# Sums of P and V of four tiles in one slot, with four buffers of transposed P, and the second attention's next y turned ahead of the output projection

## The reference

```python
x = x + xattn(ctx_1024, _layernorm(x), mask, ...)   # 16 batches, 64 latents, 512 context rows
x = x + attn(_layernorm(x), ...)                     # differential attention within each batch
x = x + ffn(_layernorm(x), ...)                      # block-quantised to FP4, inner width 1408

# xattn, width 512, 8 heads of 64: keys and values from context and latents
q = ln @ w_q
k, v = split(concatenate([xn, ln], axis=1) @ w_kv)
attn = softmax(where(m, einsum('bhid,bhjd->bhij', q, k), -max))
out = _ln(einsum('bhij,bhjd->bhid', attn, v) @ w_out, g_o, b_o)
# attn: q and k with rotary positions, two softmaxes per head
o = o1 - lam * o2
o = o * rsqrt(mean(o*o) + EPS) * ln_w + ln_b
out = o.reshape(b, s, e) @ Wo.T
```

## Time and profile before

| | |
|---|---|
| median of 3 runs | 959.94 us (958.75, 959.94, 959.97) |
| profiled execution, its own time | 958.88 us |
| its span | 957.1 us |
| busy: PE, DVE, ACT, POOL | 942.2 (98%), 730.1 (76%), 522.4 (55%), 142.7 us (15%) |
| mean granted PE clock | 0.999 of full speed |
| chain that ended last | PE 85%, DVE 6%, ACT 4%, DMA 2% |

### The profile page before, as it was taken

How to read it: one execution, slowest core, us unless ns; L and a number is a source line. 1 busy time by engine, 2 the same in 40 slices (tenths; PEclk the granted TensorE clock), 3 DMA queues, 4 the chain that set the end, 5 groups by cost and what they waited for, 6 DMA issues and landing times.

```text
span 957.1 us, 16824 instructions
## 1 busy us (share of the span) xinstructions
PE 942.2 (98%) x6400; PEld 777.4 (81%) x6400; DVE 730.1 (76%) x1512; ACT 522.4 (55%) x1088; POOL 142.7 (15%) x175
## 2 busy tenths in 40 slices
PE   9999999999999999999999999999999999999997
PEld 8778888888888888888888888776776778888885
DVE  6636577788787887886886854778898788999985
ACT  4535777777687777777776874623343422222221
POOL 6420101101201210111012010132231100000000
PEclk9999999999999999999999999999999999999999
DMA  6687657655675565676567535090004940000000
GB/s 223 167 280 209 200 135 192 158 130 157 166 185 131 163 152 154 155 196 149 129 147 181 157 106 161 12 242 2 1 1 118 247 121 12 11 12 12 12 12 23
DMA packets 119453, 120.07 MB, mean 125 GB/s; under 512 B 47430, under 2 KB 88070, under 8 KB 117324
## 3 DMA queue, kind: packets, MB, share of 16 engines
q1 hardware_dynamic: 111980, 93.30, 37.3%
q0 software_dynamic: 6816, 24.64, 8.3%
q10 hardware_dynamic: 576, 1.05, 0.3%
HBM read 89.04 MB, written 29.93 MB: 124 GB/s over the span
## 4 chain that ended last, share of the span: by engine, by line
PE 85%; DVE 6%; ACT 4%; DMA 2%; SPq 1%; issue 1%; POOL 0%; DVEq 0%; ACTq 0%; POOLq 0%
PE ps_banks L147 21%; PE ps_banks L148 21%; PE ps_banks L149 21%; PE ps_banks L473 6%; PE ps_banks L605 4%; PE ps_banks L686 3%; PE ps_banks L755 2%; PE ps_banks L756 2%; PE ps_banks L757 2%; SPq L132 1%; DMA sb_w_out_raw<-in_w_out 1%; DMA sb_wdn<-scratch_wdn 1%; PE ps_banks L486 1%; PE ps_banks L589 1%; PE ps_banks L651 1%
## 5 line engine op out<-in xcount | busy, mean ns | idle before, releaser
L147 PE MATMUL ps_banks<-sb_zT_hi,sb_wkv_hi 128*128 128x512 f32 x256 | 104.7, 409 | 0.0
L148 PE MATMUL ps_banks<-sb_wkv_lo,sb_zT_hi 128*128 128x512 f32 x256 | 100.4, 392 | 0.0
L147 PE MATMUL ps_banks<-sb_wkv_hi,sb_zT_hi 128*128 128x512 f32 x256 | 100.4, 392 | 0.0
L149 PE MATMUL ps_banks<-sb_zT_hi,sb_wkv_lo 128*128 128x512 f32 x256 | 100.3, 392 | 0.0
L149 PE MATMUL ps_banks<-sb_wkv_hi,sb_zT_lo 128*128 128x512 f32 x256 | 100.0, 391 | 0.0
L148 PE MATMUL ps_banks<-sb_zT_lo,sb_wkv_hi 128*128 128x512 f32 x256 | 99.9, 390 | 0.0
L987 DVE CUSTOM_DVE_ANT_0 sb_probs<-ps_banks,sb_maskbias 128x576 f32<-128x576 f32 x64 | 48.2, 754 | 41.5 <-PE ps_banks L149 39.9
L936 DVE TENSOR_TENSOR sb_kfull<-ps_banks,sb_rstd_row 128x512 f32<-128x512 f32 x64 | 44.2, 690 | 44.2 <-PE ps_banks L149 44.2
L1466 ACT ACTIVATE sb_kT_hi<-sb_kfull 128x512 fp32r<-128x512 f32 x64 | 40.5, 632 | 65.2 <-DVE sb_kfull L936 64.4
L147 PE MATMUL ps_banks<-sb_wgu,sb_z_hi 128*128 128x512 f32 (+1 forms) x192 | 74.0, 385 | 0.0
L148 PE MATMUL ps_banks<-sb_wgu,sb_z_hi 128*128 128x512 f32 (+1 forms) x192 | 72.1, 376 | 0.0
(11 more groups left out here) (275 smaller groups left out, 2520.8 us busy)
## 6 DMA issues: line engine op xcount, KB each, us to landing
sb_ctx<-in_ctx SPq DMA_DIRECT2D x16, 1024.0 KB, 6.4
sb_ctxT<-in_ctx_t SPq DMA_DIRECT2D x16, 1024.0 KB, 6.1
scratch_wgu<-sb_w_both POOLq DMA_DIRECT2D x22, 512.0 KB, 5.5
sb_wgu<-scratch_wgu SPq DMA_DIRECT2D x44, 256.0 KB, 5.0
sb_wdn<-scratch_wdn SPq DMA_DIRECT2D x8, 704.0 KB, 8.5
scratch_q<-sb_a_qk POOLq DMA_DIRECT2D x8, 512.0 KB, 6.6
sb_rstd_row<-scratch_rstd SPq DMA_DIRECT2D x16, 256.0 KB, 4.3
sb_qpack<-scratch_q SPq DMA_DIRECT2D x32, 128.0 KB, 6.2
```

Source lines behind the costliest of these rows:

```text
L147: e.matmul(o, wh, xh, start=i == 0, stop=False)
L148: e.matmul(o, wh, xl, start=False, stop=False)
L149: m = e.matmul(o, wl, xh, start=False, stop=i == n - 1)
```

## The change

Five things change. The program has the same multiplications, the same DMAs, and two more memsets on POOL.

1. `weigh_v` of all four tiles of the batch before is issued in slot 3. Transposed P has four buffers, with four for the latents' part.
2. The room for them comes from other buffers: `k_full` is single, so that `scale_k` waits for the `lo_of_k` before it; the quantised weight is written over `xn`, so that step 3 instead of step 10 of the next job waits for PE's transposes; two pairs of statistics buffers are shared.
3. `out_split` (DVE, even batches) stands ahead of the quantisation steps of slot 5.
4. In the second attention `turn_y(k + 1)` moves for k = 2 to 6 from step D to the place directly ahead of `project_o`. `hi_of_y` on ACT then follows `copy_out`, `lo_of_y` on DVE follows `combine`, and ACT's `copy_qk(k, 0)` stands one step later for every k.
5. `turn_a(0)` stands behind `project(2, 0)`.

```diff
-        k_full = [sb(stage_b, f"kfull{i}", [P, S]) for i in range(2)]
+        k_full = sb(stage_b, "kfull", [P, S])
+        p_main = [None, None, sb(stage_b, "probsT2", [P, CS, P]), None]
...
-        w_q4 = sb(stage_b, "w_q4", [P, D])
+        p_main[3] = sb(stage_b, "probsT3", [P, CS, P])
...
+        w_q4 = quant_w[3]
...
@@ PE, attention()
-                    if old:
+                    if old and k != 2:
                         turn_a(k - 2)
                     if new:
                         project(k, 0)
+                    if k == 2:
+                        turn_a(0)
...
-                    if k + 1 < NT:
+                    if k < 2:
                         turn_y(k + 1)
...
+                    if old and k + 1 < NT:
+                        turn_y(k + 1)
                     yield
                     if old and k != NT:
                         project_o(k - 2)
@@ PE, batches
-                    if old and slot == 0:
-                        weigh_v(b - 1, 0)
-                        weigh_v(b - 1, 1)
                     if old and slot == 3:
-                        weigh_v(b - 1, 2)
-                        weigh_v(b - 1, 3)
+                        for n in range(C):
+                            weigh_v(b - 1, n)
@@ DVE
-                if idx >= 2:
-                    on.wait_ge(k_split, idx - 1)
+                if idx:
+                    on.wait_ge(k_split, idx)
...
-                        if step == QUANT_STEPS - 1 and job:
+                        if step == 3 and job:
                             taken(("w", job - 1))
...
                     if mid:
                         combine(k - 1)
+                    if old and k + 1 < NT:
+                        lo_of_y(k + 1)
...
+                    if t_new is not None and slot == 5:
+                        out_split(t_new)
@@ ACT, copy_p and copy_p_latents
-                if idx >= 2:
-                    on.wait_ge(v_weighed, idx - 1)
+                if b:
+                    on.wait_ge(v_weighed, C * (b - 1) + n + 1)
@@ ACT, attention()
                     if new:
                         copy_v_d(k)
-                        copy_qk(k, 0)
                     yield
                     if old:
                         copy_out(k - 2)
+                    if old and k + 1 < NT:
+                        hi_of_y(k + 1)
                     if new:
+                        copy_qk(k, 0)
                         copy_qk(k, 1)
```

More of the change, by code:

```diff
@@ L216, in perceiver @@
         lam = sb(ctx, "lam", [P, 8])
-        small_z = ln_small(ctx, "e", NT)
         small_o, small_y = ln_small(ctx, "lo", NT), ln_small(ctx, "ly", NT)
-        small_b = ln_small(ctx, "b", CS)
+        small_z = (small_y[0], sb(ctx, "e_mv", [P, NT, 2]), sb(ctx, "e_ve", [P, NT]), sb(ctx, "e_rstd", [P, NT]))
+        small_b = (small_o[0], sb(ctx, "b_mv", [P, CS, 2]), sb(ctx, "b_ve", [P, CS]), sb(ctx, "b_rstd", [P, CS]))
         rstd_b = sb(ctx, "rstd_b", [P, 2, CS])
@@ L269, in perceiver @@
         probs = [sb(stage_b, f"probs{i}", [P, S + LQ]) for i in range(2)]
-        p_t = [sb(stage_b, f"probsT{i}", [P, CS + 1, P]) for i in range(2)]
+        p_whole = [sb(stage_b, f"probsT{i}", [P, CS + 1, P]) for i in range(2)]
         mask_in = [sb(stage_b, f"mask{i}", [P, S], U8) for i in range(2)]
@@ L283, in perceiver @@
         quant_w = quant_small(stage_b, "wq4", D)
+        w_q4 = quant_w[3]
         rstd_row = sb(stage_b, "rstd_row", [P, S])
+        p_latent = [sb(stage_b, f"probsT_l{i}", [P, P]) for i in (2, 3)]
+        p_main = [p[:, 0:CS, :] for p in p_whole] + [p[:, :, :] for p in p_main[2:]]
+        p_latent = [p[:, CS, :] for p in p_whole] + [p[:, :] for p in p_latent]
         stage_b.close()
@@ L301, in perceiver @@
         w_d_lo[0], w_d_lo[1] = (sb(stage_d, f"dw{n}_lo", [P, C, D], F32R) for n in "qk")
-        y = [sb(stage_d, f"y{i}", [P, D]) for i in range(2)]
+        y = [sb(stage_d, "y0", [P, D]), None]
+        leave(2048)
         w_d_lo[2] = sb(stage_d, "dwv_lo", [P, C, D], F32R)
@@ L310, in perceiver @@
         e_sb = [sb(stage_d, f"e_sb{i}", [P, 2 * H, LQ]) for i in range(2)]
-        leave(2048)
+        y[1] = sb(stage_d, "y1", [P, D])
         w_d_hi[0] = sb(stage_d, "dwq_hi", [P, C, D], F32R)
@@ L592, in weigh_v @@
             def weigh_v(b, n):
-                i, j = b % 2, n % 2
+                i = b % 2
                 on.wait_ge(drained[took["p", b, n][0]], took["p", b, n][1])
@@ L604, in weigh_v @@
                         value = vl_pack[i][:, vs] if k == CS else v_sb[i][:, k, vs]
-                        m = e.matmul(o_space(r, n), value, p_t[j][:, k, r], start=k == CS, stop=k == CS - 1)
+                        p = p_latent[n][:, r] if k == CS else p_main[n][:, k, r]
+                        m = e.matmul(o_space(r, n), value, p, start=k == CS, stop=k == CS - 1)
                 m.then_inc(v_weighed)
@@ L933, in scale_k @@
                 on.wait_ge(w_folded, 2 * C)
-                if idx >= 2:
-                    on.wait_ge(k_split, idx - 1)
-                e.tensor_tensor(k_full[n % 2][:, :], psum[:, bank, :], rstd_row[:, :], ALU.mult).then_inc(drained[bank])
+                if idx:
+                    on.wait_ge(k_split, idx)
+                e.tensor_tensor(k_full[:, :], psum[:, bank, :], rstd_row[:, :], ALU.mult).then_inc(drained[bank])
             def lo_of_k(b, n):
-                split_lo(k_full[n % 2][:, :], k_hi[:, n, context_keys], k_lo[:, n, context_keys], k_hi_done, C * b + n + 1, k_split)
+                split_lo(k_full[:, :], k_hi[:, n, context_keys], k_lo[:, n, context_keys], k_hi_done, C * b + n + 1, k_split)
             def batch_stats(b):
@@ L1371, in vector_program @@
                         lo_of_z(b + 1, slot - 4)
-                    if t_new is not None and slot == 5:
-                        out_split(t_new)
                     if cur and slot < 4:
@@ L1545, in hi_of_k @@
                     on.wait_ge(scored, C * (b - 1) + n + 1)
-                copy(k_hi[:, n, context_keys], k_full[n % 2][:, :], k_hi_done)
+                copy(k_hi[:, n, context_keys], k_full[:, :], k_hi_done)
             def copy_v(b, k):
@@ L1567, in copy_p @@
             def copy_p(b, n):
-                j, idx = n % 2, C * b + n
                 bank = taken(("p", b, n))
-                if idx >= 2:
-                    on.wait_ge(v_weighed, idx - 1)
-                copy(p_t[j][:, 0:CS, :].rearrange("p c n -> p (c n)"), psum[:, bank, :], drained[bank])
+                if b:
+                    on.wait_ge(v_weighed, C * (b - 1) + n + 1)
+                copy(p_main[n].rearrange("p c n -> p (c n)"), psum[:, bank, :], drained[bank])
             def copy_p_latents(b, *tiles):
@@ L1576, in copy_p_latents @@
                 for j, n in enumerate(tiles):
-                    if C * b + n >= 2:
-                        on.wait_ge(v_weighed, C * b + n - 1)
-                    m = e.activation(p_t[n % 2][0:LQ, CS, :], psum[0:LQ, bank, j * P:(j + 1) * P], ACT.Copy)
+                    if b:
+                        on.wait_ge(v_weighed, C * (b - 1) + n + 1)
+                    m = e.activation(p_latent[n][0:LQ, :], psum[0:LQ, bank, j * P:(j + 1) * P], ACT.Copy)
                 m.then_inc(drained[bank])
@@ L2017, in pool_program @@
                         zero_pack(e, 1)
-                        for i in range(2):
-                            e.memset(p_t[i][LQ:P, CS, :], 1.0).then_inc(p_zeroed)
-                        on.wait_ge(p_zeroed, 2)
+                        for p in p_latent:
+                            e.memset(p[LQ:P, :], 1.0).then_inc(p_zeroed)
+                        on.wait_ge(p_zeroed, C)
                     if b + 1 < NB and slot == 2:
```

## The result

The changed kernel takes 961.26 us (median of 20 runs, 959.83 to 963.70), the kernel before 959.78 us in 20 runs of its own. The ratio is 1.0018, 95% interval 1.0011 to 1.0026: some 1.5 us slower, inside the 0.2% that I had called no change. The profiled execution took 962.72 us, its span is 960.9.

The account below looks back on a forecast made before the run. PE, busy 98% of the span, was taken to bound the kernel. Merged sums 3.9 us slower less 2.4 us faster in the second attention gave 1.5 slower: 959.94 + 1.5 = 961.4 us, range 956.5 to 963.5.

Parts of the forecast that it names:

- The batches: Merging the sums with V in slot 3: 3.9 us slower in all, 0.6 of it in the last batch.
- Batch 1: Slot 0: PE may start at 116.15 instead of 116.90, against 1.18 paid in slot 3: 0.43 us lost.
- Odd ones: Batches 3, 5, 7, 9, 13: first key product waits for z_split, each 0.34 us longer, 1.7 us together.
- even ones: Batches 4, 6, 8, 10, 14: tile 3's transposes wait for the weight's bank, 0.30 us longer in batch 8, 1.5 together.
- The ideal gain of 0.21 a batch: One burst of sums instead of two saves PE 0.21 us a batch, 3 us over 15 batches.
- The last batch: b = 16: removing slot 0's sums gives nothing since PE waits there anyway; slot 3 gains 1.18 of work: 0.6 us slower.
- `turn_a(0)`: Second attention: the projection of q fills PE's wait for a_row, gaining 1.77 us.
- Tiles 2 and 3: Second attention, turn_y ahead of the output projection: 0.41 us gained each, 0.82 together, between 0.2 and 0.9.
- Tiles 4 to 7: Second attention: no gain in tiles 4 to 6, where POOL's rope_sum goes first; new places cost 0.2 us in tiles 5 to 7.
- Rival 1: The covers hold: DVE's chain runs ahead with PE, batches gain 0.21 each, 5.0 us less, 954.9; chance 0.12.
- Rival 2: POOL goes first in tiles 2 and 3, PE waits 0.26 twice: 2.0 us slower, 961.9; chance 0.16.
- Rival 3: Half the stalls: semaphores sooner or DVE's chain moving, each typical batch breaks even, 958.2; chance 0.16.

Follow-up runs that it names:

- e3_drains_first: The change with DVE's lo_of_weight moved forward in slot 0 and lo_of_z(3) in slot 7 of even batches: 958.18 us, 1.7 under the kernel before.
- e6_three_drains: e3_drains_first plus ACT's hi_of_weight ahead of hi_of_k in odd batches and DVE's invert_sum ahead of mask_row: 957.59 us, 3.4 under the kernel before.
- e1_sums_back: The change with the sums with V of tiles 0 and 1 back in slot 0: 956.73 us, 3.1 under the kernel before.
- e9_split_drains_early: The change with sums of tiles 0 and 1 back in slot 0, drains moved forward, POOL's rope_sum behind scale_out: 955.99 us, 4.2 under the kernel before.
- e5: The change with POOL's rope_sum waiting for scale_out in tiles 2 to 7 and PE turning the next y first: 962.10 us, 1.1 over the kernel before.
- e4_last_batch_split: The change with the sums of tiles 0 and 1 of the last batch alone back in slot 0: 959.34 us, 0.5 under the kernel before.
- all repairs together: The change with sums in two places in batches 1 and 16, three drains moved forward, POOL's rope_sum behind scale_out: 954.06 us, 6.9 under the kernel before.
- e2_attention_back: The change with its edits of the second attention undone: 963.97 us, 4.1 over the kernel before.
- e11_turn_a_alone: The kernel before with turn_a(0) behind the projection of q of tile 2 as only edit: 957.91 us, 2.3 under the kernel before.
- e8: The change with sums of tiles 0 and 1 back in slot 0, POOL's rope_sum behind scale_out, no drain moved: 957.04 us, 3.9 under the kernel before.
- e10: e1_sums_back with the last batch's four sums together in slot 3: 958.84 us, 1.35 under the kernel before.

## Why the prediction was right, and where not

The time of 961.4 was forecast, 961.26 came. The mechanism of every large term was found where it was expected. Yet the agreement to 0.1 us is luck: the order of work was forecast 0.8 us too slow, and a clock term of about the same size was missing.

**The batches, forecast +3.3 up to batch 15 (3.9 less the last batch's 0.6), measured +2.96.** Batch 1 0.43 as forecast. Odd ones 1.45 against 1.7, even ones 1.61 against 1.5, batches 11 and 12 -0.03 against 0.1, batches 2 and 15 -0.50 against -0.42. The waits stand at the two instructions and in the ten batches that were named. Odd ones lose a little less because DVE isn't quite as late: before the change the quantisation step ahead of `zT_lo` followed a pause of 0.10 us in each of them, and now of 0.03. It is the step whose wait for PE's transposes has moved to step 3; that this is the reason is read from the code, not tested. That the sums covered DVE's drains was argued from the trace before; `e3_drains_first` and `e6_three_drains` show it.

**The ideal gain of 0.21 a batch** is confirmed by the even batches with repaired drains (0.12 to 0.19). In odd ones it is 0.32 to 0.39. The distance from transposes to keys is 0.46, not 0.51, which explains 0.05 of it; another 0.01 to 0.07 odd batches gain in `e1_sums_back` and `e9_split_drains_early` too, without any merging. Up to 0.1 stays open. Batch 5 stays at 0.05, since there the bank of transposed P is late as well (a wait of 0.30 in `e3_drains_first`).

**The last batch at full clock, forecast +0.6, measured +0.55** (key tile 3 to the first product of v: 30.81 us in `e3`, `e5` and `e6`, 30.27 before). But "removing them gives nothing" was an incomplete sentence. It left 1.3 us of idle time in one piece, and behind it the granted clock fell in some executions. The profile of before showed its granted clock near 1.00 throughout, with an idle time of 1.61 us for `a_row`; nothing in it pointed to the fall. This is the term that was missing.

**`turn_a(0)`, forecast -1.77, measured -1.83** (scores of tile 1 at +3.32, transposes of y ahead of it at +5.15). **Tiles 2 and 3, forecast -0.41 each, measured -0.53 and -0.57**: the transposes of `o_raw` follow without a gap too. **Tiles 4 to 7, forecast 0 and +0.2 for `lo_of_y`, measured +0.08.** Together -2.85 against -2.4.

**Sum.** 2.96 + 0.55 - 2.85 = 0.7 us from the order of work, where 1.5 was forecast. The medians differ by 1.5. The other 0.8 are the clock, as an average over runs that have the stretch and runs that don't. The runs agree: by their mean clocks the 20 of the change hold 19 stretches (nine with one, five with two), the 70 of the kernel before 26, so 0.6 more in a run, and at 1.56 us each that is 0.9 (an estimate). `e4_last_batch_split`, which has the change's batches and hardly a stretch, agrees too: 959.44 at full clock, and 0.55 more is the change's 959.98.

**The rivals.** Rival 1 (the covers hold, 954.9) is refuted by the ten waits; its price was right, for with the drains early the same gains appear: in `e6_three_drains`, which differs from the change by these moves alone, the trace sums to 5.1 us under before at full clock, against the 5.0 of the rival. Rival 2 (POOL first in tiles 2 and 3) didn't happen: DVE needs no semaphore of POOL there and was ahead by 0.17 (649.29 against 649.46). In the mirror image in tile 2 `scale_out`, now first, takes its plain 0.68 and POOL's sum 1.66 in place of 1.28: the later one waits and the earlier one isn't slowed. That is exclusion and not shared bandwidth; `e5_scale_first` shows the same at a third pair of instructions. The Trainium skill (SBUF — State Buffer, "Who interferes with whom") says that such a pair contends and that issue order decides who blocks, and these traces agree. Rival 3 (half the stalls, 958.2) is refuted: they came nearly in full, 0.23 to 0.43 us a batch against 0.34 and 0.30.

## What to carry to other kernels

A piece of work that looks like overhead may be the cover of another engine's drain. Before it is moved, take each wait that follows it and subtract: when would the engine get there, and when is the thing ready now. If it is late, move the drain first, then the work. Here the moved drains turn a loss of 2.5 us in batches 2 to 15 into a gain of 3.3. (The -6.9 of all repairs together holds more: the changed second attention, the first and last batch left as they were, and POOL's order.) And a removed instruction that "gives nothing, since the engine waits there anyway" may leave the idle time in one piece: look at the granted clock behind it in more than one execution.

## What the hardware showed unasked

- A PE idle time of 1.32 and 0.30 us, 0.96 us apart, was followed in three profiles of six by some 3.4 us at 1.2 GHz, costing 1.56 us. The waits of 0.33 to 0.35 and 1.41 us near the end, 2 us apart, were followed by such a stretch in five profiles of 13. A single idle time of such a length was not followed by one: not the 1.61 us for `a_row`, before and in `e2_attention_back`, and not the 1.12 to 1.75 us ahead of the program's first P in six other profiles. What decides between runs of the same kernel stays open.
- Idle time in brackets understates a wait: 0.26 and 0.28 shown, 0.5 lost.
- The start of the program, up to the first P, varies from profile to profile and shifts all that follows. Key tile 3 of batch 1 begins 0.77 us later than in the profile of before in `e11_turn_a_alone`, whose work up to there is the same, and 0.9 to 2.1 later in `e1`, `e8`, `e9` and `e10`, whose batches are as long as before. Only distances from batch 1 on could be compared between profiles.
